# A two-layer fused kernel: its last projection in two fp16 parts, the additions of expert rows in other steps, and the gathers spread out

## The reference

```python
out = jnp.einsum('bhqk,bkhd->bqhd', attn, v).reshape(b, s, d)
out = out @ out_w.T + out_b
...
    ye = y @ w2[e].T + b2[e]
    we = jnp.sum(routing * (top_idx == e), axis=-1)
    out = out + ye * we[:, None]
...
g = _silu(_L1_ffn_ref(xn, ...))
x = x + s * g
```

## Time and profile before

| | us |
|---|---|
| median of 3 runs | 846.91 |
| lowest and highest run | 841.86 and 848.41 |
| the profiled execution | 845.22 |
| its span, first to last instruction | 843.4 |
| busy in it: TensorE | 714.2 (85%) |
| VectorE | 585.0 (69%) |
| ScalarE | 476.7 (57%) |
| GpSimd | 156.5 (19%) |

### The profile page before, as it was taken

The page is one execution under the profiler, slowest core; times in us unless marked ns, Lnnn a source line. Parts: engine busy times, 40 slices in busy tenths (PEclk is TensorE's granted clock), DMA queues, the critical chain, the costliest instruction groups (busy, mean ns, idle before and its releaser), DMA issues.

```text
span 843.4 us, 14515 instructions
## 1 busy us (share of the span) xinstructions
PE 714.2 (85%) x5342; PEld 335.0 (40%) x5342; DVE 585.0 (69%) x1190; ACT 476.7 (57%) x990; POOL 156.5 (19%) x297
## 2 busy tenths in 40 slices
PE   3477788868889998999998899989999988988885
PEld 1244454433334444444443444444444432333333
DVE  5999776598677766776777677767767777874121
ACT  2277767641566656655656555556556566546551
POOL 1422350047500001001000100010000007620111
PEclk9689989875799999999999999999999998769998
DMA  9710326534352532353247325322522412320001
GB/s 296 253 39 0 94 70 194 185 128 151 141 113 62 120 112 70 87 127 81 71 133 138 88 74 118 106 70 84 126 85 70 125 56 83 106 114 1 26 26 50
DMA packets 76994, 85.84 MB, mean 102 GB/s; under 512 B 34313, under 2 KB 60428, under 8 KB 76556
## 3 DMA queue, kind: packets, MB, share of 16 engines
q1 hardware_dynamic: 71114, 74.05, 30.9%
q0 software_dynamic: 3280, 8.98, 3.4%
q10 hardware_dynamic: 2530, 1.89, 0.8%
HBM read 39.56 MB, written 27.53 MB: 80 GB/s over the span
## 4 chain that ended last, share of the span: by engine, by line
PE 58%; ACT 15%; DVE 9%; issue 7%; DMA 4%; POOL 3%; SPq 2%; ACTq 2%; POOLq 0%; DVEq 0%
PE bank L1534 16%; PE bank L1470 8%; ACT PR L802 7%; PE bank L1432 7%; PE bank L1493 5%; PE bank L1442 5%; PE bank L1304 4%; PE bank L1549 4%; DVE PM L1203 3%; PE bank L1347 2%; PE bank L1575 2%; DMA OPS<-qk_parts 2%; ACT U L791 2%; POOL XT L567 2%; ACTq L783 2%
## 5 line engine op out<-in xcount | busy, mean ns | idle before, releaser
L802 ACT ACTIVATE PR<-bank 128x512 f32<-128x512 f32 (+3 forms) x640 | 317.6, 537 | 253.6 <-PE bank L1493 146.7
L1203 DVE TENSOR_REDUCE PM<-bank 128x1 f32<-128x512 f32 (+3 forms) x640 | 354.6, 603 | 74.4 <-PE bank L1470 46.9
L1493 PE MATMUL bank<-OPS 57*128 57x512 f16 (+3 forms) x640 | 211.8, 368 | 52.9 <-ACT PR L802 47.1
L1470 PE MATMUL bank<-OPS 54*128 54x512 f16 (+3 forms) x640 | 198.1, 379 | 11.6 <-DVE PM L1203 8.2
L1534 PE MATMUL bank<-PR,VS 128*17 128x512 f32 (+3 forms) x1280 | 164.0, 565 | 0.0
L1493 PEld LDWEIGHTS bank<-OPS 57*128 57x128 f16 x640 | 52.9, 94 | 119.4 <-ACT PR L802 110.3
L1470 PEld LDWEIGHTS bank<-OPS 54*128 54x128 f16 x640 | 50.3, 96 | 119.5 <-DVE PM L1203 75.1
L535 POOL TENSOR_TENSOR NP<-NM,NIL 128x8 bf16<-128x8 f32 x32 | 7.6, 239 | 462.2 <-DVE NM L1211 462.0
L1432 PE MATMUL bank<-WB 128*128 128x256 f16 x552 | 80.6, 275 | 0.0
L1432 PEld LDWEIGHTS bank<-WB 128*128 128x128 f16 x552 | 46.4, 101 | 35.9 <-issue 29.4
L1503 PE MATMUL bank<-MASK 64*128 64x64 bf16 x512 | 59.7, 199 | 0.0
(11 more groups left out here) (179 smaller groups left out, 780.6 us busy)
## 6 DMA issues: line engine op xcount, KB each, us to landing
WB<-W SPq DMA_DIRECT2D x23, 512.0 KB, 3.5
OPS<-qk_parts SPq DMA_DIRECT2D x60, 192.0 KB
x_rows<-PR SPq DMA_DIRECT2D x23, 256.0 KB, 3.2
WB<-in_w SPq DMA_DIRECT2D x23, 256.0 KB, 3.5
y_rows<-XT SPq DMA_DIRECT2D x23, 256.0 KB, 2.7
W<-in_w SPq DMA_DIRECT2D x6, 512.0 KB, 7.5
XT<-in_b SPq DMA_DIRECT2D x23, 128.0 KB, 3.7
XO<-in_x SPq DMA_DIRECT2D x4, 512.0 KB, 12.8
```

The lines of the kernel that those rows point to most:

```text
L802: act.activation(PR[:, tile % RING, off:CH], PS[2 + tile % 2][:, off:CH], ACT.Exp, scale=1 / SCORE).then_inc(b_exped, 1)
L1203: dve.tensor_reduce(PM[:, c % 2, j, xq, gg:gg + 1], bank[:, 0:width], AX.X, ALU.max).then_inc(a_reduced, 1)
L1470: last = mm(bank[:, 0:width], OPS[ROWS_A, slot, 0, P * (TC * a + xq):P * (TC * a + xq) + P], OPS[ROWS_A, slot, 1, CH * gg:CH * gg + width] ...
L1493: last = mm(bank[:, off:CH], OPS[ROWS_B, slot, 1, P * k:P * k + P], OPS[ROWS_B, slot, 0, CH * b + off:CH * b + CH], start=True, stop=k < T ...
```

## The change

Three things change. The output weight of the second layer is split once into two fp16 parts (`WOP`, scaled by 16), and each transposed tile into two fp16 parts (`TQ`), so that a tile has six fp16 products in place of two fp32 ones; the low part of the tile is a new VectorE step, `end_low`, between ScalarE's copy and the products. The additions move from steps 576 to 621 into steps 630 to 675, and the gathers have 16 buffers, in the memory of `W1`, and a table of steps of their own. And GpSimd's list is now written by step: the maxima, the copies of head values and the gathers in the order of their steps, from step 44 on, with all scatters that are left ahead of that.

```diff
-ADD_AT = {FIRST_BLOCK + EVERY * BLOCKS + 24 + 3 * n: t
+ADD_AT = {TOTAL - 10 + 3 * n: t
           for n, t in enumerate([2 * q + r for q in END_PAIRS for r in range(2)])}
-GATHERS = 5
+GATHERS = NT
+GATHER_AT = {PER_PAIR * (PAIRS - 1) + 4 + 4 * n: n for n in range(NT)}
+VALUES_AT = {PER_PAIR * p + LEAD + LAG + 3: p for p in range(1, PAIRS - 1)}
...
-        GB = xt32[:, 1024:1024 + 512 * GATHERS].rearrange("p (g a d) -> p g a d", g=GATHERS, a=2)
+        GB = W1[:, :, :].rearrange("p a n -> p (a n)").bitcast(F32).rearrange("p (g a d) -> p g a d", g=GATHERS, a=2)
...
-                    if n >= GATHERS:
-                        pool.wait_ge(y_added, n - GATHERS + 1)
...
             maxima(1)
-            scatter(range(6, 11))
-            maxima(2)
-            scatter(range(11, NT))
-            maxima(3)
...
+            scatter(range(6, NT))
+
+            for n in range(LEAD, STEPS):
+                ended = ends_of(n) if n < TOTAL else None
+                if ended is not None:
+                    maxima(ended)
+                if n in VALUES_AT:
+                    p = VALUES_AT[n]
                     pool.wait_ge(pv_done, PER_PAIR // QUADS * p)
                     head_values(2 * p + 2)
                     head_values(2 * p + 3)
-                maxima(NC * p + 3)
+                if n in GATHER_AT:
+                    gather(GATHER_AT[n])
...
             rows_high(NC - 1)
+            act.activation(WOP[:, 0, :, :], WO1[:, :, :], ACT.Copy, scale=WS).then_inc(wo_high, 1)
...
                 dve.wait_ge(brow_in, 16 * 4)
+                dve.tensor_scalar(BRW[D // 8:D // 4, :], BRW[D // 8:D // 4, :], WS, None, ALU.mult).then_inc(bias_part, 1)
...
+            def out_weights_low():
+
+                dve.wait_ge(wo_high, 1)
+                dve.scalar_tensor_tensor(WOP[:, 1, :, :], WO1[:, :, :], WS, WOP[:, 0, :, :], ALU.mult, ALU.subtract)\
+                    .then_inc(wo_low, 1)
+
+            def end_low(n):
+
+                dve.wait_ge(ot_copied, n + 1)
+                dve.tensor_tensor(TQ[:, n % 2, 1, :], end_banks(n)[0][:, :], TQ[:, n % 2, 0, :], ALU.subtract)\
+                    .then_inc(ot_low, 1)
...
+                if n == TOTAL:
+                    out_weights_low()
...
+                if n - 2 in END_AT:
+                    end_low(END_AT[n - 2])
...
             for n in range(len(END_AT), NT // 2):
                 end_gate(n)
+                end_low(n)
                 end_product(n)
...
             def end_project(n):
 
                 wait(pe, fin_b, n - 1)
-                pe.wait_ge(ot_copied, n + 1)
+                if n == 0:
+                    pe.wait_ge(wo_low, 1)
+                pe.wait_ge(ot_low, n + 1)
...
                     for k in range(KK):
-                        last = mm(o, TQ[:, n % 2, P * (2 * k + t):P * (2 * k + t) + P], WO1[:, k, :],
-                                  start=False, stop=k == KK - 1)
+                        for w, q in ((0, 0), (1, 0), (0, 1)):
+                            last = mm(o, TQ[:, n % 2, q, P * (2 * k + t):P * (2 * k + t) + P], WOP[:, w, k, :],
+                                      start=False, stop=k == KK - 1 and q == 1)
```

More of the change, by code:

```diff
@@ L135, in build @@
         WO1 = sb("WO1", [P, KK, D])
+        WOP = sb("WOP", [P, 2, KK, D], F16)
         POSR = sb("POSR", [ROWS8, 2, S], F16)
@@ L207, in build @@
         TAB = pr32[:, S + D:S + D + E * NT + 8 + 24 + E * E]
-        TQ = YT[:, 0]
+        TQ = YT[:, 0].rearrange("p k n -> p (k n)").bitcast(F16).rearrange("p (m j n) -> p m j n", m=2, j=2)
         KVC = YT[:, 0]
@@ L305, in build @@
             sem("fin_x"), sem("x1_in"), sem("out_st"))
+        wo_high, wo_low, ot_low = sem("wo_high"), sem("wo_low"), sem("ot_low")
         opa_in = [sem("opa_in0"), sem("opa_in1")]
@@ L558, in scatter, with gather @@
                             in_=XT[:, t % TC // 2, t % 2, CH * (t // TC):CH * (t // TC) + CH], in_offset=None).then_inc(x_scattered, 16)
-            def gather(first, last):
-                for n in range(first, last):
-                    t = list(ADD_AT.values())[n]
-                    if n >= GATHERS:
-                        pool.wait_ge(y_added, n - GATHERS + 1)
-                    for a in range(2):
-                        pool.indirect_dma_start(
-                            out=GB[:, n % GATHERS, a, :], out_offset=None, in_=y_rows,
-                            in_offset=bass.IndirectOffsetOnAxis(ap=SLOT[:, a, t:t + 1], axis=0)).then_inc(
-                                y_gathered[n % GATHERS], 16)
+            def gather(n):
+                if n == 0:
+                    for par in range(2):
+                        pool.wait_ge(y_stored[par], 16 * ((BLOCKS + 1 - par) // 2))
+                t = list(ADD_AT.values())[n]
+                for a in range(2):
+                    pool.indirect_dma_start(
+                        out=GB[:, n, a, :], out_offset=None, in_=y_rows,
+                        in_offset=bass.IndirectOffsetOnAxis(ap=SLOT[:, a, t:t + 1], axis=0)).then_inc(y_gathered[n], 16)
             pool.wait_ge(sorting, PLACED)
@@ L577, in _ @@
             maxima(1)
-            scatter(range(6, 11))
-            maxima(2)
-            scatter(range(11, NT))
-            maxima(3)
-            for p in range(1, PAIRS):
-                if p == PAIRS - 1:
-                    for par in range(2):
-                        pool.wait_ge(y_stored[par], 16 * ((BLOCKS + 1 - par) // 2))
-                    gather(0, 3)
-                maxima(NC * p)
-                if p == PAIRS - 1:
-                    gather(3, 8)
-                maxima(NC * p + 1)
-                if p == PAIRS - 1:
-                    gather(8, NT)
-                maxima(NC * p + 2)
-                if 1 <= p < PAIRS - 1:
+            scatter(range(6, NT))
[5 more added lines that the diff above has]
+                    p = VALUES_AT[n]
                     pool.wait_ge(pv_done, PER_PAIR // QUADS * p)
@@ L1122, in add_experts @@
                 place = list(ADD_AT).index(n)
-                dve.wait_ge(y_gathered[place % GATHERS], 32 * (place // GATHERS + 1))
-                dve.tensor_scalar(ACC[:, t, :], GB[:, place % GATHERS, 0, :], WTS[:, 0, t:t + 1], None, ALU.mult)\
+                dve.wait_ge(y_gathered[place], 32)
+                dve.tensor_scalar(ACC[:, t, :], GB[:, place, 0, :], WTS[:, 0, t:t + 1], None, ALU.mult)\
                     .then_inc(half_added, 1)
                 dve.wait_ge(half_added, place + 1)
-                dve.scalar_tensor_tensor(ACC[:, t, :], GB[:, place % GATHERS, 1, :], WTS[:, 1, t:t + 1],
+                dve.scalar_tensor_tensor(ACC[:, t, :], GB[:, place, 1, :], WTS[:, 1, t:t + 1],
                                          ACC[:, t, :], ALU.mult, ALU.add).then_inc(y_added, 1)
@@ L1559, in end_turn @@
                     pe.wait_ge(a_reduced, TOTAL)
-                wait(pe, ot_copied, n - 1)
+                wait(pe, ot_low, n - 1)
                 for k in range(KK):
```

17 lines of the change are left out of this document (9 added, 8 removed).

## The result

The changed kernel takes 851.33 us in the median of 16 executions (846.13 to 863.39), the kernel before in the same sitting 844.11 (837.73 to 848.41). The ratio is 1.0077, 95% interval 1.0050 to 1.0103, so 6.5 us slower (4.2 to 8.7). Forecast were 844.1 and a gain of 1.1. An execution's mean granted clock goes with its time: it is 0.911 over the 16, against 0.925 over 110 of the kernel before. That is some 152 us at half clock against some 126 (an estimate: twice what the clock lacks to 1, times the time).

What follows compares the result with a forecast made beforehand. TensorE held 58% of the chain that ended last, ScalarE and VectorE most of the rest. The terms 5.5 - 0.9 - 1.1 - 4.1 + 1.2 - 3.2 + 1.3 + 0.2 = -1.1 took 845.2 us to 844.1, range 836 to 855.

Steps and rivals of the forecast that it cites:

- 1. Scatters: Pair 0, turn of chunk 2: ten more scatters ahead of the maxima make TensorE stop, +5.5 us.
- rival (b): Half clock lasts from 712 to 763 in the last pair (854.8), or follows pair 0's stop (853.1); chance 0.12.
- 2. Gathers: Last pair: with a buffer for each gather, TensorE's waits at chunks 28 and 30 go, -0.9 us.
- 3. Additions out of the first pass: Last pair: VectorE freed of additions, -1.1 us from 729 to 742.7 and -4.1 in the second half-clock stretch.
- rival (a): Last pair: second half-clock stretch stays, since missing expert matmuls starve TensorE, not the additions; 848.2 us, chance 0.20.
- (c): Last pair: with gathers and additions away, the first clock fall at 712 does not happen either; 835.3 us, chance 0.14.
- 4. Additions in the last ten steps: Steps 630 to 639: four additions on VectorE, 3.1 us, nearly fit its idle 2.9; cost +1.2 us.
- The other twelve free: After step 639: the remaining twelve additions, 9.4 us, fall where VectorE has idle time and cost nothing.
- 5 to 7. Projection, tail and preparations: Second layer's projection -3.2 us (shorter products -4.8, waits +0.75 and +0.85), tail +1.3, preparations +0.2.
- The tail: Last two pairs of tiles: pair 7's low part stands behind pair 6's product on VectorE, +1.3 us.
- The preparations: Ahead of a pass: one ScalarE copy (0.60 us) and one tiny VectorE operation for the biases, +0.2 us.
- (d): Pair 0: no stop, as TensorE comes later to the turn of chunk 2; 838.6 us, chance 0.09.

Runs made afterwards that it cites:

- additions_only: The kernel before with only the new gathers and the additions moved out of the first pass: 839.60 us, ratio 0.9926.
- additions_cut: As additions_only, with the twelve additions of the second pass of the last chunks left out: 839.40 us, ratio 0.9937 against the kernel before.
- projection_only: The kernel before with only the new projection (six fp16 products, low part on VectorE included): 849.95 us, ratio 1.0062.
- fp16_products_only: As projection_only, without the low part and its wait, the high part's products repeated in its place: 843.10 us, ratio 0.9985 against the kernel before.
- scatters_only: The kernel before with the twenty scatters of pair 0 in one row, nothing else changed: 852.09 us, ratio 1.0100.

## Why the prediction was wrong

It forecast a gain of 1.1 us, and 6.5 were lost; the range held. By its steps:

**1. Scatters, forecast +5.5, measured +8.4 (6.0 to 10.9): mechanism right, undersized.** The stop is there, at the turn named, 5.43 us long. The sum left out what comes behind it. The prediction had this as the second place of rival (b), 23 steps at half clock for +9.0 on top of the stop. The trace has half clock there from 220.4 to 244.3, the stop included, and against the 14 profiles without a stop pair 0 takes 57.0 - 46.3 = 10.7 us more: some 5 beyond the stop in the profiles, 3 in the timing. That half clock is what these are, the fillers did not confirm: with the stop filled, pair 0 still takes 7.9 us more.
The Trainium skill (TensorE: Matmul & The Clock Gate, section What's actually happening) says that activity releases the throttled state. The trace agrees with its direction: from a stop without work on there are 17 to 24 us at half clock, at one filled with matmuls 3 to 7, no more than before without a stop. By it the fillers should also have given time back, and the medians (851.9 and 852.5 against 852.1) do not show that.

**2. Gathers, -0.9: right in kind.** No turn of the last pair waits for GpSimd. What that alone is worth was not measured.

**3. Additions out of the first pass, -5.2: right mechanism, undersized.** The last pair's first pass takes 9.2 us less in the mean of the profiles (64.4 against 73.6). The second stretch at half clock shrank or went, as forecast, and in all but the changed kernel's profile the first one did too, in which no change was forecast. The two stretches of the earlier trace rows were no fixed state to start from: of the ten profiles with additions as before, five have only one, of 17 to 24 us. In additions_only the windows of the reduction show the whole of it, 72 steps in 59.6 us at 0.91, where before (second row) 76 took 73.5 at 0.74:

```profile
700.00:759.60 59.60, 40.48 (x72) 0.91 0.33 103
```

```profile
700.00:773.50 73.50, 42.81 (x76) 0.74 0.27 86
```

So rival (a), that the missing expert products starve TensorE, falls, and (c) is true of the first pass.

**4. Additions in the last ten steps, +1.2: measured 0.** Ten steps take as long as before; windows of the reduction from step 630 on, 8.6 us wide, the changed kernel's ahead of that of before:

```profile
766.70:775.30 8.60, 5.92 (x11) 1.00 0.00 0
```

```profile
765.00:773.60 8.60, 5.92 (x11) 1.00 0.00 0
```

From step 630 to step 640 it is 8.56 us in the mean in both groups of profiles. "The other twelve free" is shown by additions_cut. But steps 640 to 683 take 4.2 us more in the mean of the profiles where the additions were moved (55.4 against 51.2). The ranges overlap; among the kernels without the low part they do not: 56.3 to 56.9 in four, 47.5 to 53.6 in six. That gives back half of item 3, and 9.2 - 4.2 = 5.0 is, by luck in the parts, near the forecast 4.9 of items 2 to 4 and inside the measured 6.2 (3.6 to 8.8). What lowers the clock there stays open: neither the twelve additions nor the four in steps 630 to 639 bring the fall by themselves.

**5 to 7. Projection, tail and preparations, forecast -3.2 + 1.3 + 0.2 = -1.7, measured +5.2 (3.1 to 7.3): this is the step that failed.** Three of its terms did.
The saving of a tile was put at 0.40 and is 0.30 (1.27 less 0.97). It set 0.11 us for an fp16 product, from a row of the expert blocks, against 0.53 for an fp32 one. The 0.11 holds here too: behind the first, the six products start 0.109 apart. But from the first of them to the next tile's bias product it is 0.76 us (826.37 to 827.13), since some 0.1 lie behind the last one, which the row of the expert blocks doesn't have. And the 0.53 has such gaps in it: the trace has two records for each fp32 product, which start 0.216 apart within a tile behind the first, so 0.43 for a product.
The Trainium skill (FP8 and Floating Point Precision, section TensorE Precision Notes) gives true fp32 four passes. Four of 0.109 are 0.44, and the records give 0.43: the trace agrees, and what the prediction held against the rule was its own reading of 0.53.
With 0.30 the eight pairs would save 4.8, where the prediction's 0.40 makes 6.4 (six pairs 4.8, the tail 1.6). Measured without the low part was 1.3 (up to 3.1). In that run's profile the tail gives nothing back, since its four tiles run at half clock.
The waits were put at 0.75 and 0.85 beside the second pass and at some 2 between the last two pairs, and the trace has 0.97, 0.78 and 2.14: their lengths are right. Their price is more, 6.5 us by difference and 10.5 (7.3 to 13.7) alone, with fp32 products behind them. The clock is a part of it as far as the tail goes; for the second pass that is not shown.
The tail was worked out at full clock. Its mechanism is right: the second low part stands behind the first product, and TensorE waits 2.14 us for it. But in projection_only its four tiles take 1.69 instead of 0.97 us each, 2.9 more. Over the profiles this tail takes 26.0 us against 22.0 without the low part, and the ranges are apart: 4.0 more, where 1.3 were forecast. Turning the order on VectorE gives back 2.4 of them in the profiles. Half clock in the tail does not need these waits, though: fp16_products_only, additions_only and scatters_only have it too.
The preparations cannot be seen: the first reduction starts at 181.8 us instead of 183.1, and between 180.0 and 185.2 over all the profiles.

**Rivals.** (d), no stop, is refuted. (b) came nearest in time (853.1, for its place in pair 0) at a chance of 0.12, but not for its reason alone: pair 0 cost less than it said, and the projection the rest. No rival had steps 640 to 683 and the tail lose clock. In the profiled execution these two take 15 us more than before, pair 0 10.8 more, and the last pair 7.7 less. The sum priced the waits and products there at the full clock, by a profile that showed 0.97.

## What to carry to other kernels

When TensorE bounds a stage, price a new wait in its list not only at its own length: here waits of the length forecast cost more than that. Work out what stands behind them at both levels of the clock and keep the second as the upper end. Take a group's time from rows of the same place, start to start over one whole tile: six products 0.109 us apart took 0.76 to the start of the next tile, not 0.66. Before merging rows of work on a slow queue, compare when the result behind them is wanted with when it would come: ten scatters of 1.26 us against 7.1 us of slack was the whole stop.

## What the runs showed of the hardware that was not expected

The granted clock differs between executions of one program on one core: 0.888 to 0.925 over the 16 of the changed kernel, and the time goes with it, 863.39 and 846.13 us at those two.
The clock can fall in work that did not change. In scatters_only steps 640 to 683 are the kernel before's, and took 53.6 us in its profile instead of 48.9.
Work on VectorE that halved, from 20.77 to 9.36 us, left a stage of 56.4 us and its clock as they were.
An fp32 product of 128x128 by 256 columns stands in the trace as two records 0.216 us apart, and an fp16 one as one of 0.109: the fp32 one costs four times as much.
